# A top-2-of-8 expert layer in a graph block: tokens turned by a transposing DMA, and the second layer's waits placed elsewhere in TensorE's stream

## The reference

```python
xn = _layernorm(x)                                   # (6250, 256)
gate_scores = einsum('bsd,ed->bse', xn, Wg) + bg     # 8 experts
topk_scores, topk_idx = jax.lax.top_k(gate_scores, 2)
topk_probs = softmax(topk_scores)
combine = sum(topk_probs[..., None] * one_hot(topk_idx, 8), axis=-2)
out = zeros_like(xn)
for e in range(8):
    h = relu(einsum('bsd,hd->bsh', xn, W1[e]) + b1[e])   # 256 -> 1024
    y = einsum('bsh,dh->bsd', h, W2[e]) + b2[e]          # 1024 -> 256
    out = out + combine[..., e:e + 1] * y
x = x + out
```

## Time and profile before

| | us |
|---|---|
| median of 3 runs | 2081.33 (2079.99 to 2083.32) |
| the profiled execution | 2084.09 |
| its span, first to last instruction | 2082.3 |
| TensorE busy in the span | 1682.2 (81%) |
| VectorE busy | 1575.3 (76%) |
| ScalarE busy | 1429.4 (69%) |
| GpSimd busy | 1290.2 (62%) |

### The profile page before, as it was taken

How to read it: one execution, slowest core, us unless ns; L and a number is a source line. 1 busy time by engine, 2 the same in 40 slices (tenths; PEclk the granted TensorE clock), 3 DMA queues, 4 the chain that set the end, 5 groups by cost and what they waited for, 6 DMA issues and landing times. The chain is left out here.

```text
span 2082.3 us, 51199 instructions
## 1 busy us (share of the span) xinstructions
PE 1682.2 (81%) x15514; PEld 1312.3 (63%) x15514; DVE 1575.3 (76%) x3299; ACT 1429.4 (69%) x4059; POOL 1290.2 (62%) x1229
## 2 busy tenths in 40 slices
PE   5677728888888789888986666572899999999998
PEld 2456626676666577777774344342677777777776
DVE  8899718888888899998998988887355555555554
ACT  6565418888888778887878888675565665665554
POOL 3488847777777777777777777650344444444443
PEclk9899869999999999999999999855899999999999
DMA  6122235555555554444433346461222222222321
GB/s 218 33 79 79 76 113 174 157 155 154 158 158 150 157 150 124 124 123 121 126 107 102 102 150 184 127 207 33 56 48 50 48 47 47 48 48 48 50 48 29
DMA packets 140382, 219.02 MB, mean 105 GB/s; under 512 B 32086, under 2 KB 97536, under 8 KB 140002
## 3 DMA queue, kind: packets, MB, share of 16 engines
q0 software_dynamic: 62816, 134.68, 25.6%
q1 hardware_dynamic: 70950, 74.70, 11.7%
q10 hardware_dynamic: 6364, 6.40, 0.9%
HBM read 172.28 MB, written 44.36 MB: 104 GB/s over the span
## 5 line engine op out<-in xcount | busy, mean ns | idle before, releaser
L1009 POOL DMA_INDIRECT misc<-z_d,consts x814 | 783.7, 963 | 271.9 <-issue 161.3
L1245 DVE SCALAR_TENSOR_TENSOR acc<-ps,consts,acc 128x512 f32 x814 | 609.1, 748 | 79.8 <-PE ps L1332 62.9
L1032 ACT ACTIVATE misc<-misc 128x256 f16<-128x256 f16 x872 | 391.6, 498 | 82.6 <-DVE misc L1112 76.0
L1839 ACT ACTIVATE misc<-ps,misc 128x128 f32<-128x128 f32 x840 | 240.1, 368 | 238.5 <-PE ps L1804 164.9
L1330 PE MATMUL ps<-misc 128*128 128x256 f16 x1088 | 297.8, 274 | 123.8 <-ACT rec L1032 46.1
L1880 POOL DMA_INDIRECT out<-misc,pos x105 | 166.2, 1583 | 289.7 <-ACT misc L1904 250.8
L1804 PE MATMUL ps<-misc,big 128*128 128x128 f16 x1680 | 327.6, 220 | 0.0
L1802 PE MATMUL ps<-misc,big 128*128 128x128 f16 x1680 | 327.2, 220 | 0.1
L1803 PE MATMUL ps<-misc,big 128*128 128x128 f16 x1680 | 327.0, 220 | 0.0
L1819 PE MATMUL ps<-big,rec 128*128 x840 | 319.7, 381 | 0.0
L1332 PE MATMUL ps<-misc 128*128 128x256 f16 x1088 | 298.6, 274 | 0.0
(11 more groups left out here) (348 smaller groups left out, 3780.0 us busy)
## 6 DMA issues: line engine op xcount, KB each, us to landing
big<-in_w2T SPq DMA_DIRECT2D x60, 256.0 KB, 2.9
misc<-z_d,consts POOLq DMA_INDIRECT x814
big<-xT_d SPq DMA_DIRECT2D x98, 128.0 KB
big<-in_w1T SPq DMA_DIRECT2D x32, 256.0 KB, 3.0
tok_d<-misc SPq DMA_DIRECT2D x50, 132.0 KB, 1.8
xT_d<-misc SPq DMA_DIRECT2D x49, 128.0 KB
z_d<-misc SPq DMA_DIRECT2D x49, 128.0 KB, 1.7
acc<-in_x SPq DMA_DIRECT2D x6, 896.0 KB
```

Of the source, the lines that this page charges most:

```text
L1009: e.indirect_dma_start(out=rows[n % RB], out_offset=None, in_=c.z_d, in_offset=bass.IndirectOffsetOnAxis(ap=idx[u][:, k:k + 1], axis=0)).t ...
L1032: e.activation(hot[n % HG][:, half, :], same[n % OG], ACT.Copy, scale=near[n // UG % 3][:, t % UG, 1 + half:2 + half]).then_inc(s_hot, 1)
L1245: e.scalar_tensor_tensor(out=rows_of, in0=out_ps[tile % BG], scalar=c.gain, in1=rows_of, op0=ALU.mult, op1=ALU.add).then_inc(s_add, 1)
L1839: l = e.activation(hidden[:, m, :], h_ps[u][:, m, :], ACT.Relu, bias=b1x[u][:, m:m + 1])
```

## The change

- The rows of a tile are turned by a DMA that SyncE issues (`dma_start_transpose`), from the gathered rows straight into `xT`; TensorE's `turn`, its PSUM tiles, the semaphores `s_tr` and the single `s_xt`, and ScalarE's copy are gone. SyncE waits for the gather of the tile and, from the fifth tile on, for the first layer of the tile four back (`s_h`).
- `xs` and `xT` have four buffers each (`XB`) instead of two, and lie in `c.acc`, which is free in this stage. A gather from the fifth on waits for the transpose of the tile four back and for the copy of that tile's shares.
- `first(m = 0)` waits for the DMA's semaphore of its buffer; it had waited for ScalarE's copy. ScalarE's copy of the shares waits for the gather itself.
- `second` has no waits in front of its wide product. A new function `ready` issues the waits of a block right behind the wide product of the block before it: those of m = 0 (`s_low`, and `s_t` from the third tile on) behind the wide product of m = 7 of the preceding tile, that of m = 4 between the wide and the 256-column product of m = 3. For the first tile it is called by itself. `s_out` is signalled by the same product as before.

```diff
--- before.py
+++ after.py
@@ -1751,9 +1751,11 @@
 
     misc, more = Arena(c.misc, MISC), Arena(c.rec, REC)
     more.t = c.rec[:, :].bitcast(F32)
-    xs = [misc.take(ROW, F16) for _ in range(2)]
-    xT = [matrix(misc.take(2 * D, F16), 2 * DH, P) for _ in range(2)]
-    b2 = c.acc[:, 0:NE * D]
+    XB = 4
+    spare = Arena(c.acc, NB * BR * D // P)
+    b2 = spare.take(NE * D)
+    xT = [matrix(spare.take(2 * D, F16), 2 * DH, P) for _ in range(XB)]
+    xs = [spare.take(ROW, F16) for _ in range(XB)]
     shares, weight = [misc.take(NE) for _ in range(2)], [misc.take(1) for _ in range(4)]
     y, y2 = ([misc.take(D) for _ in range(2)] for _ in range(2))
     b1 = misc.take(NE * HB)
@@ -1762,11 +1764,11 @@
     more.at = NT * NE
     high, low = ([matrix(more.take(H, F16), HB, P) for _ in range(2)] for _ in range(2))
     S = lambda name: c.sem("experts_" + name)
-    s_b, s_bias, s_bx, s_tr, s_xt, s_h, s_relu, s_high, s_low, s_out, s_y2, s_y = map(S, (
-        "b1", "bias", "b1_x", "tr", "xt", "h", "relu", "high", "low", "out", "y2", "y"))
+    s_b, s_bias, s_bx, s_h, s_relu, s_high, s_low, s_out, s_y2, s_y = map(S, (
+        "b1", "bias", "b1_x", "h", "relu", "high", "low", "out", "y2", "y"))
     AHEAD, LAG = 6, HB + HB // 2
-    s_xs, s_ys, s_t, s_p, s_wt, s_b2 = [S("xs0"), S("xs1")], [S("ystore0"), S("ystore1")], S("sum"), S("shares"), S("weight"), S("b2")
-    tr_ps = [matrix(c.bank[u][:, 0:D].bitcast(F16), 2 * DH, P) for u in range(2)]
+    s_xs, s_xt = [S(f"xs{k}") for k in range(XB)], [S(f"turned{k}") for k in range(XB)]
+    s_ys, s_t, s_p, s_wt, s_b2 = [S("ystore0"), S("ystore1")], S("sum"), S("shares"), S("weight"), S("b2")
     h_ps = [matrix(c.wide[1 + u], HB, P) for u in range(2)]
     y_ps = [c.bank[6], c.bank[7]]
     half = HB // 2
@@ -1780,47 +1782,44 @@
             skip_runtime_bounds_check_because="a count of at most NE - 1 ends")
         return x
 
-    def turn(e, i):
-        u = i % 2
-        e.wait_ge(s_xs[u], 16 * (i // 2 + 1))
-        if i >= 2:
-            e.wait_ge(s_xt, i - 1)
-        for n in range(2 * DH):
-            l = e.transpose(tr_ps[u][:, n, :], xs[u][:, n * P:n * P + P], c.ident16)
-        l.then_inc(s_tr, 1)
-
     def first(e, i, x, m):
 
         u = i % 2
         if m == 0:
-            e.wait_ge(s_xt, i + 1)
+            e.wait_ge(s_xt[i % XB], 16 * (i // XB + 1))
         if i >= 2 and m % half == 0:
             e.wait_ge(s_relu, 2 * i - 3 + m // half)
         o = h_ps[u][:, m, :]
         for h in range(DH):
             at = bass.ds(x * H + (h * NE * H + m * P), P)
-            e.matmul(o, w1h[:, at], xT[u][:, h, :], start=h == 0, stop=False)
-            e.matmul(o, w1h[:, at], xT[u][:, DH + h, :], start=False, stop=False)
-            l = e.matmul(o, w1l[:, at], xT[u][:, h, :], start=False, stop=h == DH - 1)
+            turned = xT[i % XB]
+            e.matmul(o, w1h[:, at], turned[:, h, :], start=h == 0, stop=False)
+            e.matmul(o, w1h[:, at], turned[:, DH + h, :], start=False, stop=False)
+            l = e.matmul(o, w1l[:, at], turned[:, h, :], start=False, stop=h == DH - 1)
         if m % half == half - 1:
             l.then_inc(s_h, 1)
 
+    def ready(e, n):
+
+        i, m = n // HB, n % HB
+        if i < MT and m % half == 0:
+            e.wait_ge(s_low, 2 * i + 1 + m // half)
+        if i < MT and m == 0 and i >= 2:
+            e.wait_ge(s_t, i - 1)
+
     def second(e, i, x, m):
 
         u = i % 2
-        if m % half == 0:
-            e.wait_ge(s_low, 2 * i + 1 + m // half)
-        if m == 0 and i >= 2:
-            e.wait_ge(s_t, i - 1)
         at = x * (2 * D) + m * NE * 2 * D
         if m == HB - 1:
             e.matmul(y_ps[u][:, 0:D], low[u][:, m, :], c.w2[:, bass.ds(at, D)], start=False, stop=False)
 
         l = e.matmul(y_ps[u], high[u][:, m, :], c.w2[:, bass.ds(at, 2 * D)], start=m == 0, stop=m == HB - 1)
+        if m == HB - 1:
+            l.then_inc(s_out, 1)
+        ready(e, i * HB + m + 1)
         if m < HB - 1:
             e.matmul(y_ps[u][:, 0:D], low[u][:, m, :], c.w2[:, bass.ds(at, D)], start=False, stop=False)
-        else:
-            l.then_inc(s_out, 1)
 
     def relu(e, i, x):
 
@@ -1862,16 +1861,23 @@
         def _(e):
             e.dma_start(b1, A["b1T"]).then_inc(s_b, 16)
             e.dma_start(b2, A["b2"].rearrange("(a e) d -> a (e d)", a=1).to_broadcast([P, NE * D])).then_inc(s_b2, 16)
+            for i in range(MT):
+                k = i % XB
+                e.wait_ge(s_xs[k], 16 * (i // XB + 1))
+                if i >= XB:
+                    e.wait_ge(s_h, 2 * (i - XB + 1))
+                e.dma_start_transpose(xT[k], xs[k][:, 0:2 * D]).then_inc(s_xt[k], 16)
             e.wait_ge(s_b2, 16)
 
         @block.gpsimd
         def _(e):
-            def gather(s):
-                if not s.fresh:
-                    e.wait_ge(s_tr, s.i - 1)
-                    e.wait_ge(s_p, s.i - 1)
-                e.indirect_dma_start(out=xs[s.u].bitcast(F32), out_offset=None, in_=c.tok_d,
-                                     in_offset=bass.IndirectOffsetOnAxis(ap=c.token[:, s.i:s.i + 1], axis=0)).then_inc(s_xs[s.u], 16)
+            def gather(i):
+                k = i % XB
+                if i >= XB:
+                    e.wait_ge(s_xt[k], 16 * (i // XB))
+                    e.wait_ge(s_p, i - XB + 1)
+                e.indirect_dma_start(out=xs[k].bitcast(F32), out_offset=None, in_=c.tok_d,
+                                     in_offset=bass.IndirectOffsetOnAxis(ap=c.token[:, i:i + 1], axis=0)).then_inc(s_xs[k], 16)
 
             def scatter(s):
                 e.wait_ge(s_y, s.i + 1)
@@ -1882,11 +1888,11 @@
                                      bounds_check=N - 1, oob_is_err=False).then_inc(s_ys[s.u], 16)
 
             for i in range(AHEAD):
-                gather(Step(i // 2, i % 2))
+                gather(i)
             for i in range(MT):
                 scatter(Step(i // 2, i % 2))
                 if i + AHEAD < MT:
-                    gather(Step((i + AHEAD) // 2, i % 2))
+                    gather(i + AHEAD)
             e.wait_ge(s_ys[0], 16 * (MT // 2 + 1))
             e.wait_ge(s_ys[1], 16 * (MT // 2))
 
@@ -1897,11 +1903,8 @@
             e.wait_ge(s_bias, 1)
             def step(i):
                 u = i % 2
-                e.wait_ge(s_tr, i + 1)
-                if i >= 2:
-                    e.wait_ge(s_h, 2 * i - 2)
-                e.copy(xT[u], tr_ps[u]).then_inc(s_xt, 1)
-                e.copy(shares[u], xs[u][:, 2 * D:ROW].bitcast(F32)).then_inc(s_p, 1)
+                e.wait_ge(s_xs[i % XB], 16 * (i // XB + 1))
+                e.copy(shares[u], xs[i % XB][:, 2 * D:ROW].bitcast(F32)).then_inc(s_p, 1)
             for i in range(MT + 1):
                 if i < MT:
                     step(i)
@@ -1940,16 +1943,15 @@
         def _(e):
             x = {}
 
-            turn(e, 0)
             for n in range(MT * HB + LAG):
                 i, m = n // HB, n % HB
                 if i < MT:
                     if m == 0:
                         if i % KNOWN == 0:
                             x.update(enumerate(known(e, mybir.EngineType.PE, i), i))
-                        if i < MT - 1:
-                            turn(e, i + 1)
                     first(e, i, x[i], m)
+                if n == LAG:
+                    ready(e, 0)
                 if n >= LAG:
                     k = (n - LAG) // HB
                     second(e, k, x[k], (n - LAG) % HB)
```

## The result

The changed kernel takes 2070.39 us (median of 6 runs, 2065.29 to 2072.75) against 2082.74 for the kernel before, measured with it: ratio 0.9937, 95% interval 0.9924 to 0.9949. That is 12.4 us faster. I had forecast 28.0 us; the sign is right, the size is not.

What follows compares the result with a forecast made beforehand. TensorE's instruction stream was taken to bound the expert stage. Turns -22.9, hole -6.0 and start +0.9 sum to -28.0 us, from 2081.33 to 2053.3; range 2048.5 to 2074, chance 0.74, the sum's own range 2050.7 to 2061.1.

Steps and rivals of the forecast that it cites:

- TensorE's stream bounds the stage: Expert stage: it lasts as long as TensorE's instruction stream, some 612 us, with TensorE busy 99.49 of 100 us.
- ScalarE's copy: ScalarE loses a copy of 0.599 us per step and two waits; claimed worth nothing, as it idles 40 of 100 us.
- latency of the transposes is hidden after the first: SyncE's transposes: four buffers cover latency, with 10 us available for a transfer needed once per 5.44 us.
- its price on the engines: One transpose on the DMA engines: 512 pieces at 55 ns, 1.76 us of all 16, share 0.29 becoming about 0.6.
- The start: Before the stage's first product, the first transpose is exposed: +0.9 us, between +0.3 and +2.7.
- 5.24 for four in series: Estimate from the skill's page for one transpose's four blocks: start costs 3.8 us more, a step just hidden.
- B: Scatter chain: transposes delay scatters, 6.4 us per step, +68, 2149 us; decides from a landing of 4.6 us; chance 0.08.
- C: Transpose throughput: small pieces give 2944 us, blocks in series 2193 to 2234; decides at 5.44 us per transpose; chance 0.08.
- D: Change has no effect: waits effectively unmoved, turns' time lost elsewhere, within 0.2% of before, 2081 us; chance 0.03.
- 103 x 0.222 = 22.9 us, all on the path: TensorE's four turning products per step, 0.222 us, removed: the full 22.9 us saved, as the stream has no idle time.
- The hole of 0.078, I take 6 us: Gap before each step's first wide second-layer product: moving waits saves 6 us, bounds 8.0 or nothing.
- Rival A: TensorE's queue, not its array, becomes the bound without the turns: 2077 us, or 2065 for half of it; chance 0.07.

Runs made afterwards that it cites:

- e7: Kernel before plus one transposing DMA per step that no engine waits for: 2086.28 against 2085.65 us for the kernel before, ratio 1.0002.
- e8: Changed kernel without the clipping waits and, by summing on VectorE before the split, without the sum wait: 2054.42 us, ratio 0.9866 to the kernel before.
- e4: Kernel before, TensorE turning, with expert 0's weights for every tile, no run-time addresses: 2061.76 against 2085.65 us for the kernel before, ratio 0.9902.
- e3: Changed kernel with expert 0's weights for every tile, no run-time addresses: 2235.91 against 2281.04 us for the kernel before, ratio 0.9801.
- e1: Changed kernel with the second layer's waits back in front of the wide products: 2269.65 against 2281.04 us for the kernel before, ratio 0.9945.
- e2: Kernel before, still turning on TensorE, with waits moved behind the wide products: 2281.05 against 2281.04 us for the kernel before, ratio 0.9997.
- e5: Changed kernel without the two waits per step on ScalarE's clipping: 2258.36 against 2281.04 us for the kernel before, ratio 0.9890.
- e6: Changed kernel with four more, long satisfied waits per step on TensorE: 2100.42 against 2085.65 us for the kernel before, ratio 1.0081.
- e12: Changed kernel with four more waits per step and fixed weight addresses (expert 0 for every tile): single run, 2258.08 us, step 5.28 us.
- e11: e8 with expert numbers loaded 15 at a time instead of 8: 2293.76 against 2301.54 us for the kernel before, ratio 0.9963.

## Why the prediction was wrong

**That TensorE's stream bounds the stage** was right, before and after the earlier trace rows. So was most that follows from it: ScalarE's copy was worth nothing, the tail is the same, and latency of the transposes is hidden after the first.

**The transposing DMA** was right in kind, and its price on the engines was put too high. The hardware queue moved 57120 packets more in 105 transposes, 544 each, where I had 512:

```profile
q1 hardware_dynamic: 128070, 88.47, 15.7%
```

The DMA share rose from 0.29 to 0.44, not to 0.6: these packets are cheaper than the 55 ns of the earlier trace rows. The start cost 1.2 us, within its bounds. The Trainium skill, "VectorE: DVE Perf Modes", section on the three transpose paths, gave 1309 ns per 128x128 block, and my estimate from it was 5.24 for four in series; this trace has the whole transpose, issue to landing, in 2.51, so that estimate does not hold here. Rivals B and C fall with it: after the change scatters land in 3.8 us, and e7 and e8 have transposes at 3.3 and 2.5 us and scatters at 4.2 and 3.9, below the 4.6 from which B decides. D, no change, is outside the interval of 0.9924 to 0.9949.

**"103 x 0.222 = 22.9 us, all on the path"** is the step that failed most. 0.222 is the right price of the array's time (e4 less e3: 0.22). But the steps shrank by 0.133, 13.3 us over the 100 measured, and e1 shows that all of this is the turns'. My reason was that "the stream has no idle time to take it up". TensorE is two things, an array and a queue that feeds it, and a busy array does not say that the queue has room. The turning products need no address arithmetic, so they give the queue work that it gets rid of faster than the array does. The hole behind their former place (0.015 before, 0.053 after) is the part of it that can be seen; it is 0.04 of the 0.089 us lost, some 0.02 is a longer hole at the register loads, the rest is scattered. That it is this cover, and not another property of those four products, is argued from e3, e4 and the place of the hole; no run put other products without arithmetic in their place. The turns also had a wait entry of their own in the queue, one of the three per step, so the products themselves gave still less than 0.133.

**"The hole of 0.078, I take 6 us"** is the other one: 0 (e2: 0.9997). I had argued that a wide product hides waits since it streams for longer. It does hide them where they stand. But they use up the lead that the queue needs for the narrow block behind, and the hole opens six products later, just where it had been. I had read the rule "waits behind a longer product cost nothing" off, where the four turning products follow and restore the lead.

**Rival A** named this mechanism and got 7 in 100. I priced it from the right rows, six narrow products in 0.56 instead of 0.33, and dismissed it since the queue "recovers within one block". The measured 2070.4 lies between its two prices, 2065 and 2077. That it also lies inside my range, 2048.5 to 2074, is no merit of the forecast: the range's own sum ended at 2061.1, and the rest of it was drawn over most of A. These rows show a queue that runs at the array's speed or below in a narrow block; the weight loads that start with their products say so too. Had I counted the queue's entries of a block as I had counted the array's products, five at 0.124 us in a block of 0.66 would have told me. The sum then is 22.9 less what stays open: with 0.089 us per step lost, 0.133 x 103 = 13.7 less the start's 1.2 gives 12.5, against the measured 12.4.

A share of busy time could not show it: TensorE is busy for 99.49 of 100 us before and 99.27 after, while the products of a step alone need 5.28 of the 5.58 us (e3), 5% less. The Trainium skill, "Perfetto Trace Analysis", says in its opening note that busy time of products is a bad metric because they are pipelined; the trace agrees.

## What to carry to other kernels

When an engine looks 99% busy, read its queue as a second resource: count the address arithmetic, waits and loads per block beside the products, and look whether weight loads start ahead of their products or together with them. Where they start together, remove entries of the queue (waits that another wait implies, addresses that can be fixed) before products, and expect a moved wait to cost what it cost. Of waits, count those that have an entry of their own. An experiment with fixed addresses prices the whole queue at once: here 0.30 us per step, more than the turns.

## What I had not expected of the hardware

- What a wait costs TensorE fits best with the entry that it needs in the queue: 0.09 (e5, e8) to 0.13 us (e6) for each `EVENT_SEMAPHORE` when the queue has no lead, and nothing when it has (e12). Counted by wait it would be 0.04 (e5), 0.07 (e6) and 0.09 (e8). No run takes out a lone wait, one without an entry, by itself.
- A load of 15 registers takes 3.85 us and one of 8 takes 0.59 (medians of e11 and e8). The Trainium skill, "DMA: Bandwidth & Descriptors", section on latency, has some 600 ns as the floor of such a load; the median of 0.59 for 8 agrees, the last load, of a single number, took 0.31, below it (e8), and 15 are another matter. Where between 8 and 15 the jump lies was not tried, nor why two of the seven loads of 15 took under 2 us.
- In e11 the three steps after such a load take 5.28 us each, without any hole, though their address arithmetic and waits are the same as in the later ones (5.32 median). The trace shows why: while the array ran at half its clock, the queue got ahead. In the first two of these steps, after each of the five long loads, it does the arithmetic of line 1796 between 1.1 and 1.4 us before the product starts; before the load and from the fourth step on it is 0.1 to 0.4. The lead goes in the third, when the queue stands still for 1.0 to 1.4 us (1800.98 to 1802.09 after the load of 1778.0) at the wait of the second layer's block 0. That VectorE is late with its signal there because of its own load (3.8 us from 1795.9) fits, and no run tests it. What keeps the queue from building such a lead at full clock, where by 0.62 of 0.66 us per block it should slowly grow, stays open.
